# Second layer of a two-layer transformer with routed experts: residual kept by token, without its mean; two centrings a layer go, two products change form

## The reference

```
xn = layernorm(x)
x = x + L0_attn(xn) + L0_ffn(xn)          # 8 dense experts, summed
xn = layernorm(x)
z = xn
for i in range(4):
    z = z + attention(layernorm(z)*ln1_w+ln1_b) @ aproj_w + aproj_b
    z = z + gelu((layernorm(z)*ln2_w+ln2_b) @ fc_w + fc_b) @ mproj_w + mproj_b
x = x + z + L1_ffn(xn)                    # top 2 of 8 experts a token
```

## Time and profile before

| | us |
|---|---|
| median of 3 executions | 1594.45 (1592.38 to 1595.95) |
| the profiled execution | 1592.25 |
| its span, first to last instruction | 1590.4 |
| PE busy | 1480.2 (93%) |
| DVE busy | 1167.9 (73%) |
| ACT busy | 1039.9 (65%) |
| POOL busy | 341.8 (21%) |

### The profile page before, as it was taken

One profiled execution on the slowest core, in us unless ns is written; L12 is line 12 of the kernel. 1 busy time (PEld: TensorE's weight loads), 2 busy tenths in 40 slices (PEclk: granted clock), 3 DMA queues, 4 the chain that ended last, 5 costly groups with the idle time before them and its releaser, 6 DMA issues.

```text
span 1590.4 us, 20945 instructions
## 1 busy us (share of the span) xinstructions
PE 1480.2 (93%) x6278; PEld 988.1 (62%) x6278; DVE 1167.9 (73%) x1414; ACT 1039.9 (65%) x2503; POOL 341.8 (21%) x251
## 2 busy tenths in 40 slices
PE   6999999999999999999999999999779999999978
PEld 4677657666556655556656655655447767877655
DVE  3434644895689869999459957998979855799495
ACT  7457547657676777767687658577766576667742
POOL 0001203111411230103111401131134432344230
PEclk9999999999999999999999999999889999999989
DMA  6754434334244434344344334351155545554433
GB/s 237 271 193 154 137 116 149 117 116 162 88 138 124 157 102 127 113 153 127 102 139 155 101 95 120 110 148 49 48 163 165 157 126 161 166 158 142 150 109 120
DMA packets 109675, 217.32 MB, mean 137 GB/s; under 512 B 13687, under 2 KB 57420, under 8 KB 108076
## 3 DMA queue, kind: packets, MB, share of 16 engines
q1 hardware_dynamic: 105020, 206.60, 41.5%
q0 software_dynamic: 4544, 9.38, 1.7%
HBM read 168.81 MB, written 39.93 MB: 131 GB/s over the span
## 4 chain that ended last, share of the span: by engine, by line
PE 43%; issue 19%; DVE 15%; ACT 15%; POOL 4%; DMA 3%; SPq 1%; POOLq 0%; ACTq 0%; DVEq 0%
PE bank L1250 6%; PE bank L1416 4%; PE bank L1238 4%; PE bank L1240 4%; PE bank L1239 4%; PE bank L1410 4%; PE bank L1328 3%; ACT ROWS L781 3%; POOL RSTD L945 2%; PE bank L1451 2%; ACT ROWS L794 2%; DVE AM L1003 2%; PE bank L1390 2%; DVE SH L1115 2%; DVE TA L999 2%
## 5 line engine op out<-in xcount | busy, mean ns | idle before, releaser
L945 POOL TENSOR_TENSOR RSTD<-SS,power_half 128x4 f32<-128x4 f32 x96 | 138.1, 1439 | 933.8 <-ACT ROWS L781 933.6
L1238 PE MATMUL bank<-NH,GU 128*128 128x512 f32 x512 | 265.7, 519 | 1.6 <-ACT SH L772 1.2
L1115 DVE TENSOR_TENSOR SH<-SH,bank 128x512 f32<-128x512 f32 x256 | 171.8, 682 | 129.0 <-ACT SH L772 89.2
L1250 PE MATMUL bank<-SH,WD 128*128 128x512 f32 x512 | 262.2, 594 | 0.0
L999 DVE TENSOR_TENSOR TA<-QK 128x2048 f32<-128x2048 f32 x96 | 219.5, 2287 | 1.3
L772 ACT ACTIVATE SH<-bank 128x512 f32<-128x512 f32 x256 | 151.4, 602 | 98.6 <-PE bank L1240 95.9
L781 ACT ACTIVATE ROWS<-bank,root_eps 128x128 f32<-128x128 f32 x384 | 135.5, 368 | 113.1 <-PE bank L1328 113.0
L1240 PE MATMUL bank<-NL,GU 128*128 128x512 f32 x512 | 205.0, 400 | 0.0
L1239 PE MATMUL bank<-NH,GU 128*128 128x512 f32 x512 | 204.0, 398 | 0.0
L1003 DVE TENSOR_TENSOR AM<-AM,TA 128x1024 f32<-128x1024 f32 x128 | 153.0, 1218 | 0.8
L1451 PE MATMUL bank<-XT,GU 128*128 128x256 f32 x624 | 145.5, 379 | 0.5 <-ACT XT L921 0.5
(11 more groups left out here) (205 smaller groups left out, 2576.2 us busy)
## 6 DMA issues: line engine op xcount, KB each, us to landing
GU<-halves SPq DMA_DIRECT2D x112, 512.0 KB
GU<-in_w_gu SPq DMA_DIRECT2D x39, 512.0 KB
xg<-in_c_fill SPq DMA_DIRECT2D x8, 2080.0 KB
WD<-in_w_d SPq DMA_DIRECT2D x128, 128.0 KB
QK<-QK SPq DMA_DIRECT2D x32, 480.0 KB
WD<-in_w_d SPq DMA_DIRECT2D x39, 256.0 KB
halves<-GU SPq DMA_DIRECT2D x8, 1024.0 KB, 8.6
FC<-ready_w SPq DMA_DIRECT2D x32, 256.0 KB
```

What stands on the lines that cost most here:

```text
L945: pool.tensor_tensor(RSTD[:], SS[:], (power_one if k[0] == "at" else power_half)[:], ALU.pow).then_inc(power_done, 1)
L1115: dve.tensor_tensor(SH[:, g % 4, :], SH[:, g % 4, :], banks[2 + g % 2][:], ALU.mult).then_inc(h_ready, 1)
L1238: pe.matmul(out, w_hi, x_hi, start=True, stop=False)
L1250: pe.matmul(banks[4][:], WD1[:, slot, :], SH[:, g % 4, :], start=first, stop=last).then_inc(down_done, 1)
```

## The change

Z now lies with tokens on partitions, 130 columns for each group of 128 tokens (`R = P + 2`): 128 features without their mean, and the mean in column 128. It starts as the output of n3's `scale`, which has no mean. What is added to it is made without a mean as well: the weights of the two last products and their biases are prepared with the mean over the output features taken out, and that mean as extra columns (`prep_mats`, `prep_wp`, `prep_low` on DVE and ACT; kept in `ready_w`, `ready_m`, `ready_b`).

- A and C have no `centre` any more. `square` on ACT reads Z itself, and so does `scale`. They hold bank 5 only for `turn` and `normed`.
- `proj` and `mproj` come out by token: for each of four groups of 128 tokens the activations are the stationary operand and the 130 weight columns the moving one. Three groups fit bank 7, the fourth goes to bank 6, so both banks are held. A float32r product of two rows (`two` with BP or BM, high and low part of the bias) starts each bank. `add_out` adds both banks to Z in two DVE instructions.
- n3: `scale` writes Z once; a new ACT step `send` copies it to SEND0 and SEND; the turned rows go to XS for `logits`.
- `total` transposes X by PE into bank 6 and adds rows, mean and X by four DVE instructions. `back` is gone; `merge` adds the two routed rows by two DVE instructions. The output is stored by token.
- All tables of numbers of the planner are set anew, so the order changes everywhere.

```diff
-             "PE": ("turn", "centre", "den", "freq", "proj", "back", "turn_in"),
+             "PE": ("turn", "centre", "den", "freq", "proj", "total", "turn_in"),
...
+        elif kind in ("A", "C"):
+            step("square", k, urgency, [(ACT_, 1.15, ("LN",))], after)
+            step("power", k, urgency, [(POOL, 1.4)], [("square", k, ACT_)])
+            step("scale", k, urgency, [(ACT_, 1.1)], [("power", k, POOL)])
...
-    EARLY = 60.0
+    EARLY = 47.74
...
-            step("proj", key, u + 1.4, [(PE, 0.86, ("7",), ("XG", "WP"))], [("gain", key, DVE), ("load_p", key, SP, 4.0)])
+            step("proj", key, u + 1.4, [(PE, 1.15, ("7", "6"), ("XG", "WP"))], [("gain", key, DVE), ("load_p", key, SP, 4.5)] + ([] if l else [("send", t, ACT_)]))
...
-                sp.dma_start(MP[:], A["w1_mproj"][k[1]]).then_inc(m_loaded, 16)
+                sp.dma_start(MP[:], ready_m[k[1]]).then_inc(m_loaded, 16)
+                sp.wait_ge(rounded_set, 3)
+                sp.dma_start(BM[:].bitcast(F32), ready_b[k[1]][:, 1, :]).then_inc(m_loaded, 16)
...
+                for i in range(GROUPS):
+                    ins = act.activation(ROWS[:, i, :], rows(t)[:, i, 0:P], ACT.Square, bias=root_eps, scale=P ** -0.5,
+                                         accum_out=SS[:, i:i + 1])
...
+                act.activation(SEND0[:, :, 0:P], rows(k)[:, :, 0:P], ACT.Copy)
+                act.activation(SEND[:, :, 0:P], rows(k)[:, :, 0:P], ACT.Copy).then_inc(sent, 1)
...
+        def add_out(t):
+            some = rows(t)[:, 0:3, :]
+            dve.tensor_tensor(some, banks[7][:, 0:3 * R].rearrange("p (g n) -> p g n", n=R), some, ALU.add)
+            some = rows(t)[:, 3, :]
+            return dve.tensor_tensor(some, banks[6][:, 0:R], some, ALU.add)
...
+                for i in range(GROUPS):
+                    row = rows(k)[:, i, :]
+                    ins = dve.scalar_tensor_tensor(row[:, 0:P], row[:, 0:P], row[:, P:P + 1], banks[6][:, i * P:(i + 1) * P],
+                                                   ALU.add, ALU.add)
...
-                dve.tensor_tensor(tile(X, k), tile(X, k), banks[k % YSLOTS][:], ALU.add).then_inc(out_ready, 1)
+                out = rows(k)[:, :, 0:P]
+                dve.tensor_tensor(out, out, YL[:, i, 0, :, :], ALU.add).then_inc(y_added, 1)
+                dve.wait_ge(y_added, n + 1)
+                dve.tensor_tensor(out, out, YL[:, i, 1, :, :], ALU.add).then_inc(out_ready, 1)
...
+        def last_product(x, w, bias):
+            for bank, groups in ((7, range(0, 3)), (6, range(3, GROUPS))):
+                m = len(groups)
+                out = banks[bank][:, 0:m * R].rearrange("p (g n) -> p g n", n=R)
+                pe.matmul(out, two[:].broadcast_to([2, P]), bias[:].unsqueeze(1).broadcast_to([2, m, R]), start=True, stop=False)
+                for c in range(x.shape[1]):
+                    for i, g in enumerate(groups):
+                        mm = pe.matmul(out[:, i, :], x[:, c, g * P:(g + 1) * P], w[:, c, :], start=False,
+                                       stop=(c == x.shape[1] - 1 and i == m - 1))
...
-                pe.matmul(banks[7][:], WP[:], XG[:], start=True, stop=True).then_inc(proj_done, 1)
+                last_product(XG[:].unsqueeze(1), WP[:].unsqueeze(1), BP).then_inc(proj_done, 1)
...
-                for c in range(4):
-                    mm = pe.matmul(banks[7][:], MP[:, c, :], GE[:, c, :], start=(c == 0), stop=(c == 3))
-                mm.then_inc(mp_done, 1)
+                last_product(GE, MP, BM).then_inc(mp_done, 1)
...
-                for g in range(GROUPS):
-                    for j in range(2):
-                        mm = pe.matmul(banks[i][:, g * P:(g + 1) * P], YL[:, i, j, g, :], ident[:], start=(j == 0), stop=(j == 1))
-                mm.then_inc(y_turned, 1)
+                for i in range(GROUPS):
+                    mm = pe.transpose(banks[6][:, i * P:(i + 1) * P], tile(X, k)[:, i * P:(i + 1) * P], ident[:])
+                mm.then_inc(x_back, 1)
```

More of the change, by code:

```diff
@@ L237, in schedule @@
             after += [("raw", 0, SP, 3.0)]
-        scaling(a + NORM0[h], "n0", (t,), after, [(ACT_, 0.5), (DVE, 0.6, (), ("LN",))])
+        scaling(a + NORM0[h], "n0", (t,), after, [(ACT_, 0.5), (DVE, 0.6, (), ("5",))])
         step("keys", t, a + KEYS[h], [(PE, 2.8, ("6", "7")), (DVE, 1.2, (), ("6", "7"))],
@@ L737, in _ @@
                 sp.wait_ge(out_ready, n + 1)
[L738 removed]
+                sp.dma_start(A["out"][k * TILE:(k + 1) * TILE, :].rearrange("(g p) n -> p g n", p=P), rows(k)[:, :, 0:P]).then_inc(out_stored, 16)
         sp.wait_ge(out_stored, 16 * TILES)
```

397 lines of the change are left out of this document (238 added, 159 removed).

## The result

The changed kernel takes 1630.95 us (median of 4 runs, 1624.1 to 1634.6), the kernel before 1593.9 (1592.4 to 1595.95, 4 runs). The ratio is 1.023, 95% interval [1.021, 1.025]: 37 us slower. Forecast were 1568 us and a range of 1540 to 1598; the result lies outside, on the other side of no change.

The account below looks back on a forecast made before the run. TensorE was taken to bound the two long stretches, a chain the short ones. Stretches of 1091 + 71 + 374 + 29 gave a 1565 us span, with time outside it and the run median 1568 us; range 1540 to 1598.

Parts of the forecast that it names:

- Where PE bounds, and what its work costs: TensorE bounds the two long stretches; centrings and "back" groups go, narrow products cost by columns: -36.5 us on PE in all.
- The bias products: Four float32r products per tile-layer in the two last products, taken by columns at 0.82 us; upper bound 1.62, eating the gain.
- the net of -26 us on PE: PE over 32 tile-layers: centrings -1.78 us each, attention projection +0.44, MLP's last product +0.52, net -0.82 each.
- My 0.085 for a change of type: Price of a switch between fp32 and float32r at each bias product, two per last product, 0.17 us together.
- To the last expert step: First stretch, 1110 us before: 19 us less PE work, unfilled 70 us kept, so 1091 us, bounds 1085 and 1100.
- To the first routed product: Second stretch, a chain from n3's centring through routing: kept at 71 us, bounds 61 and 81.
- Routed experts: Third stretch: 348 us of PE work plus the unfilled 26 of before, 374 us, bounds 364 and 395.
- The rival of DVE as the bound: Third stretch: 326 us of DVE work at 78% busy lasts 418 us, end at 1611; decides from 402 us; chance 0.12.
- The tail: Behind the last routed product, 54.4 us before: routed loads and merges beside one MLP, 29 us, bounds 26 and 34.
- The other engines: ACT reading SBUF +16 us, DVE adds +6, merges and total +11, preparation about 12; at most 5 us of wait.
- nothing gained: Rival: the saved PE work reappears as waits on ACT, POOL and the transposes, 1591 to 1597 us; chance 0.06.
- narrow products dear: Rival: 40 narrow records per tile-layer at 0.133 us each, +28 us, 1596, far more by the skill's rule; chance 0.04.

Follow-up runs that it names:

- experiment 2: The changed kernel with each bias product issued twice in a row, same result: 1646.83 us, against 1630.95 for the changed kernel.
- experiment 9: The changed kernel with bias products side by side (1604.84 us), the planner told measured durations and given new urgencies, so only the order differs: 1599.17 us.
- Experiment 8: The changed kernel with bias products side by side (1604.84 us), with VectorE's gain put one step forward at three places: 1604.57 us.
- Experiments 9 to 12: Bias products side by side, four variants: new order 1599.17 us; another order 1617.51; the first with a bias product ahead of the gain wait 1599.49; that, third order 1603.64.
- experiments 1 and 6: The changed kernel without its bias products, 1588.98 us; and that kernel with the routed experts' multiply covering 256 of 512 columns, 1579.13 us.

## Why the prediction was wrong, point by point

*Where PE bounds, and what its work costs.* Right: narrow fp32 products cost by their columns (0.111 a record), the removed centrings and "back" groups went. The Trainium skill's rule ("TensorE: Matmul & The Clock Gate", section "Back-to-back issue gap") of 81 and 131 ns, which by my estimate would have given 1740 us, doesn't hold for fp32 here: an fp32 product took 0.222 us at 130 columns and 0.86 at 512.

*The bias products: the term that failed.* Forecast 0.82 us per tile-layer "by columns", measured 1.62, the stated upper bound. With 19 tile-layers ahead of the last expert step, 11 among the routed experts, 1.5 between and half a one behind, that is 15 + 9 + 1 us of the 67 missed, and it alone turns the net of -26 us on PE into none. The choice was the fault: of two ends I took the one by columns, "since an fp32 record of 512 columns costs four times one of 128". That row is of products of 128 rows in a dense run; it says nothing of a single product of two rows between them. My 0.085 for a change of type was misread as well: the 0.32 us run from the first float32r product's own start, and that start lies 0.03 us behind the last fp32 record's, not 0.111, so the change in that row costs nothing (experiment 2). So my 0.17 for each last product counted something that is free, and the 0.37 of the borders beside the two rows stood in no row of the kernel before; the prediction said that no row shows such products. The pair side by side (-26 us) and the double (+16) show that the price goes by the neighbours: 0.37 of 0.81 us are the borders, 0.2 the loads.

*To the last expert step*, 1091 forecast, 1133 measured. 15 of the 42 us are the bias products. A count without prices: PE is busy for 10 us more than before where I forecast 19 less, 29 in all, and stands 72 us in place of 60. So beside the 15 us there are 14 more of busy time and 13 of waits. The 14 go with half clock: 55 us of it here, 17 before, and PE, which was busy in 52 and 17 of them, loses half of that, up to 18 us. A second reading of what half clock costs: over ten runs of experiment 9's kernel, one and the same order, the granted clock went from 0.969 to 0.980 and the time from 1602.6 to 1592.9 us, 0.9 us for 0.001. The profiled executions have 0.982 before and 0.960 after (the lowest of its four runs): by that 20 us over the whole kernel, and some 10 for the first stretch's share of the half clock. My sum had no term for it: the unfilled 70 us of before were carried over with the clock and the waits of before in them. What makes the clock fall stays open. Ahead of the last expert step it fell ten times, eight of them 2 to 5 us after PE began to stand for 2.1 to 4.2 us, as here behind the stand of 3.6 us at 425,

```profile
421.00:428.00 7.00, 4.21 (x13) 2.10 (x12) 6.55 (x21) 3.62 (x7) 0.00 (x0) 1.00 0.45 156
428.00:434.80 6.80, 6.04 (x17) 4.80 (x18) 4.78 (x7) 1.32 (x6) 0.00 (x0) 0.52 0.23 69
```

but two of the falls had no such stand ahead of them, and two stands of 2.0 and 2.4 us no fall behind. Experiment 8 cut three stands to 1.3 us; the half clock near 425 went, that near 725 stayed, and some came in other places. The bias products' part in it isn't settled: the first stretch had 38 us of half clock without them, and 38 too with them side by side, but the clock of the whole kernel hardly moved: without them it was 0.964 to 0.971 over five runs, with them 0.960 to 0.967 over four. The order seems to have a part (experiment 9: 14 us of half clock and a stretch of 1092), though the same order with a moved product had 31.

*To the first routed product*, 71 forecast, 85 measured, outside the bounds (81). I had seen that the last tile's FFN end and n2 step were put behind the last expert step, gave 5 us for it and set them against a scaling pass less. PE in order of time:

```profile
1133.68 2.81 PE L1496 MATMUL bank<-raw,WDA 128*128 128x512 f32 x6 [1.08 <-DVE raw L1269]
...
1139.28 1.16 PE L1447 MATMUL bank<-centre,attn_raw 128*128 128x128 f32 x8 [0.75 <-ACT XS L900]
...
1154.72 1.51 PE L1447 MATMUL bank<-centre,X 128*128 128x128 f32 x8 [0.69 <-ACT XS L900]
```

The centring of n3 starts 22 us behind the last expert step (10 before; 15 forecast), then 64 us to the first routed product (62 before). FFN end, n2 and n3 are three links of one chain, each through PE, ACT, POOL and DVE, and mostly at half clock (56 of 86 us; the stretch's clock is 0.67, 0.81 before). Experiments 9 to 12 have it at 72 to 73 us with the new layout and other orders, so it is the order, not the layout.

*Routed experts*, 374 forecast, 386 measured: 9 of the 12 us are the bias products. The rival of DVE as the bound didn't come: the stretch stayed under 402 us. DVE ran at 81%, though, where the forecast asked for 87% and the signs that I had named for 85%; it was busy for 312 us, not the 326 that I had priced. And experiments 1 and 6 show it close behind: with PE relieved by 18 us, 13 of them did not come back. My 374 left no room for that.

*The tail*, 29 forecast, 28.8 measured, by the mechanism named: loads at +5, DVE's merges in the order of landing, the last MLP beside them.

```profile
1604.75 1.88 PE L1532 MATMUL bank<-XS,FC 128*128 128x512 f32 x4
...
1609.48 5.17 SPq L788 DMA_DIRECT2D YL<-ytok  x8
...
1629.36 0.69 DVE L1341 TENSOR_TENSOR Z<-Z,YL 128x512 f32<-128x512 f32 x1
```

The routed loads landed in 4.8 us (3.9 before) and the stores in 4.5 (2.4), with stores and loads in flight together. The last three merges waited 0.95 us each for their loads, and the eighth began at +24 where I had its load land at +22, so that the sum met to 0.2 us is in part luck.

*The other engines.* ACT's square and scale cost 393 and 392 ns from SBUF (365 and 371 from a bank), 256 x 0.049 = 13 us where I had 16; the adds 0.562 + 0.282 = 0.844 us (0.84 forecast), the total 0.342 an instruction (0.35), merges 0.69 (0.69). The preparation made no one wait: its loads landed in 6.3 and 8.1 us. All as forecast, and harmless.

*The chances.* The rivals had "nothing gained" at 0.06 and "narrow products dear" at 0.04, both ending near 1596. The case that came, the bias products at their upper bound and an order with more half clock and a longer second stretch, was in no rival; the slower side had only DVE and half of the narrow products' 0.04 as mechanisms and the bound that should have been another was left as a footnote of the sum.

## What to carry to other kernels

A small product of two rows in a dense stream of 128-row products is priced by its neighbours, not by its columns: here two borders of 0.09 us and a whole weight load of 0.10. Put such products side by side. Before you price a change from the distance between two starts, look at the start of the record ahead as well: it may have been early. When a sum takes one end of a range whose other end eats the whole gain, that other end is a rival with a chance of its own. And when a layout changes durations, the order made for the old ones is part of the cost; read the clock of each stretch before carrying its unfilled time over.

## What the runs showed of the hardware

- A float32r product of 2 rows between fp32 products of 128 rows costs its columns, about 0.10 us of weight load and 0.09 at either border, the same for 130 and 390 columns. Its load record starts with it and not, as for products of 128 rows, with the product ahead.
- Between products of 128 rows the change from fp32 to float32r and back costs nothing: 0.347 us over a 128-column fp32 record and a 512-column float32r product (0.111 + 0.235), and 0.236 for a float32r product before an fp32 one.
- GpSimd adds 520 fp32 elements a partition in 1.8 to 1.9 us on average, and DVE's 1024-element products of two SBUF operands took 1867 ns where they overlapped such an addition, 1220 where not.
- One order of one kernel varied from 1592.9 to 1602.9 us between runs, with the granted clock from 0.980 to 0.969.
